# An attention and mixture-of-experts kernel: the experts' rows normalised by GpSimd, turned through memory in 32-column quarters and VectorE's 32x32 transposes, and the first matrices kept on chip

## The reference

```python
x = x + attn(layernorm(x))          # 16 heads, squared scores, causal in chunks of 64, a running state
x = x + ffn(layernorm(x))

# ffn: 8 experts, the best two of the softmax are weighed, but the higher-numbered of them wins
scores = softmax(x @ gate_w + gate_b)
wf = the two largest scores of a token, at their experts, else 0
for i in range(8):
    h = relu(xf * wf[:, i:i+1] @ w1[i] + b1[i])       # w1[i]: 128 x 512
    y = h @ w2[i] + b2[i]                             # w2[i]: 512 x 128
    out = where(wf[:, i:i+1] > 0, y, out)
```

## Time and profile before

| | us |
|---|---|
| median of three runs | 279.69 |
| the profiled run | 279.19 |
| span of its profile | 277.1 |
| PE busy in the span | 256.0 |
| DVE busy | 180.3 |
| ACT busy | 170.3 |
| POOL busy | 165.4 |
| first product of the experts starts | 192.24 |
| granted clock of TensorE, mean | 1.0 of full |

### The profile page before, as it was taken

One profiled execution on the slowest core, in us unless ns is written; L12 is line 12 of the kernel. 1 busy time (PEld: TensorE's weight loads), 2 busy tenths in 40 slices (PEclk: granted clock), 3 DMA queues, 4 the chain that ended last, 5 costly groups with the idle time before them and its releaser, 6 DMA issues.

```text
span 277.1 us, 9167 instructions
## 1 busy us (share of the span) xinstructions
PE 256.0 (92%) x3141; PEld 205.8 (74%) x3141; DVE 180.3 (65%) x726; ACT 170.3 (61%) x297; POOL 165.4 (60%) x190
## 2 busy tenths in 40 slices
PE   0969999999999999999999999788999999999993
PEld 0757677677767777777777777555899899999993
DVE  5472453794776498399299479768878855555552
ACT  2366676767666767676767676564565565656550
POOL 6074444563668596686674775782287775545454
PEclk9999999999999999999999999999999999999999
DMA  5789999999600000000000000065676479877400
GB/s 149 217 297 311 358 361 358 356 332 359 229 21 12 12 22 4 19 22 2 22 13 11 22 7 15 22 190 147 155 225 178 120 187 263 251 214 191 147 31 8
DMA packets 31580, 40.58 MB, mean 146 GB/s; under 512 B 3330, under 2 KB 24356, under 8 KB 31536
## 3 DMA queue, kind: packets, MB, share of 16 engines
q1 hardware_dynamic: 29264, 35.76, 42.7%
q0 software_dynamic: 2272, 4.25, 4.4%
HBM read 17.98 MB, written 22.48 MB: 146 GB/s over the span
## 4 chain that ended last, share of the span: by engine, by line
PE 60%; SPq 22%; DMA 5%; ACT 4%; DVE 3%; issue 3%; POOL 2%; ACTq 0%; DVEq 0%; POOLq 0%
PE sc L1015 24%; PE av L1015 17%; SPq L336 15%; PE p L1015 15%; DMA expert_rows<-pad_rows 5%; ACT scores L402 4%; PE p L1018 4%; SPq L314 3%; SPq L330 2%; POOL expert_rows L553 1%; POOL out L566 1%; POOL scores L528 0%; DVE logit L721 0%; DVE stats L697 0%; SPq L328 0%
## 5 line engine op out<-in xcount | busy, mean ns | idle before, releaser
L402 ACT ACTIVATE scores<-sc 128x1536 f32<-128x1536 f32 x64 | 92.9, 1451 | 48.4 <-PE sc L1015 48.4
L528 POOL TENSOR_SCALAR_AFFINE_SELECT scores<-scores 128x1024 f32<-128x1024 f32 x64 | 70.7, 1107 | 46.3 <-ACT scores L402 46.0
L1015 PE MATMUL sc<-q_sb,k_sb 32*128 32x256 f32 (+1 forms) x1024 | 59.8, 347 | 6.8 <-ACT scores L402 5.6
L1015 PEld LDWEIGHTS sc<-q_sb,k_sb 32*128 32x128 f32 x1024 | 46.3, 184 | 22.1 <-ACT scores L402 15.4
L566 POOL DMA_INDIRECT out<-y_sb,xr x39 | 38.7, 993 | 26.7 <-DVE y_sb L956 20.1
L1015 PE MATMUL av<-scores,v_ext 128*32 128x256 f32 (+1 forms) x1024 | 48.9, 329 | 1.0 <-POOL scores L528 0.8
L475 ACT ACTIVATE hT<-sc,b_sb 128x128 f32<-128x128 f32 x78 | 24.5, 364 | 32.8 <-PE sc L1015 32.7
L553 POOL DMA_INDIRECT expert_rows<-rows,slot_i x32 | 32.2, 1008 | 19.8 <-DVE slot_i L805 9.5
L660 DVE TENSOR_SCALAR k_sb<-p,parity 128x512 f32<-128x512 f32 x32 | 22.5, 744 | 32.4 <-PE p L1015 32.4
L1015 PE MATMUL sc<-xwT,w_t 128*128 128x128 f32 x312 | 41.4, 276 | 0.0
L1015 PEld LDWEIGHTS av<-scores,v_ext 128*32 128x32 f32 x1024 | 28.5, 109 | 16.7 <-POOL scores L528 1.6
(11 more groups left out here) (136 smaller groups left out, 330.3 us busy)
## 6 DMA issues: line engine op xcount, KB each, us to landing
expert_rows<-pad_rows SPq DMA_DIRECT2D x11, 1572.0 KB, 17.8
w_t<-in_L_ffn_w SPq DMA_DIRECT2D x39, 256.0 KB, 3.5
xr<-expert_rows SPq DMA_DIRECT2D x39, 65.5 KB, 3.1
rows<-in_L_attn_hidden_states SPq DMA_DIRECT2D x16, 128.0 KB, 2.7
out<-y_sb,xr POOLq DMA_INDIRECT x39, 3.4
b_sb<-in_L_ffn_b SPq DMA_DIRECT2D x1, 512.0 KB, 5.1
expert_rows<-rows,slot_i POOLq DMA_INDIRECT x32, 2.4
wk_sb<-in_L_attn_Wk SPq DMA_DIRECT2D x1, 128.0 KB, 2.8
```

What stands on the lines that cost most here:

```text
L402: nc.scalar.activation(scores[g][:, :, :, :].rearrange("p c a t -> p c (a t)"), sc[:, :, 0:SW], ACT.Square, scale=Q_SCALE).then_inc(square ...
L528: nc.gpsimd.affine_select(out=scores[g][:, :, 0:2, :], in_=scores[g][:, :, 0:2, :], compare_op=ALU.is_ge, fill=0.0, base=0, pattern=[[0, G ...
L1015: return nc.tensor.matmul(o, lhsT=l, rhs=r, start=start, stop=stop)
```

## The change

- The rows are normalised by POOL (`normalise`, now `tensor_scalar`, with 7 buffers `xw`). POOL does tiles 0 to 5 ahead of its late scatters, and then tile t + 6 after the result of tile t.
- SP stores each normalised tile to a new table `turned` in external memory, as four quarters of 32 features (`store_rows`: 128 x 4 pieces of 128 bytes). Once that has landed, SP loads it back with 32 rows by 4 blocks on each partition (`load_blocks`: 128 pieces of 512 bytes). The load of tile t stands behind the store of tile t + 1.
- DVE turns the tile with one transpose of 32x32 blocks (`turn`), two tiles ahead, between `begin_y` and `late_piece`.
- PE's transposes of the rows and ACT's normalising and copying of them are gone.
- One DMA of 2 MB loads all first matrices (`w1_sb`), ahead of the pads. ACT copies the expert's matrix into one of three buffers `w1_t` (`copy_w1`), two tiles ahead.
- `LEAD`, the number of row loads ahead in the second wave, goes from 4 to 6.

```diff
-    XR, W1, Y, XWT = 20, 6, 10, 4
+    XR, W1, Y, XWT, XW, XB = 20, 3, 10, 4, 7, 6
+    turned = nc.dram_tensor("turned_rows", (TILES, D // STRIP, P, STRIP), fp32, kind="Internal").ap()
...
+            sp.dma_start(w1_sb[:, :].rearrange("p (e n) -> p e n", e=E), w1.rearrange("e d n -> d e n")).then_inc(moe_w, 16)
             sp.dma_start(b1_rows[:, :], b1.rearrange("e (c f) -> (e c) f", f=P)).then_inc(moe_w, 16)
...
-            def load_w1(t, e):
-                after(sp, up_done, t - W1 + 1)
-                sp.dma_start(w1_t[t % W1][:, :], w1[bass.ds(e, 1)].rearrange("e d n -> d (e n)")
-                             ).then_inc(w1_in[t % W1], 16)
...
+            def store_rows(t):
+                sp.wait_ge(xw_ready, t + 1)
+                sp.dma_start(turned[t].rearrange("a q j -> q a j"),
+                             xw[t % XW][:, :].rearrange("q (a j) -> q a j", j=STRIP)).then_inc(xw_out[t % XW], 16)
+            def load_blocks(t):
+                sp.wait_ge(xw_out[t % XW], 16 * (t // XW + 1))
+                after(sp, xwT_ready, t - XB + 1)
+                sp.dma_start(xb[t % XB][:, :],
+                             turned[t].rearrange("a (i b) j -> (a i) (b j)", i=STRIP)).then_inc(xb_in[t % XB], 16)
...
             for t in range(WAVE):
                 load_rows(t, row[t])
-                if t in (3, 5):
-                    load_w1((t + 5) // 2, e[(t + 5) // 2])
-            for t in range(W1, WAVE):
-                load_w1(t, e[t])
+            for t in range(WAVE):
+                store_rows(t)
+                if t:
+                    load_blocks(t - 1)
+            load_blocks(WAVE - 1)
...
                     load_rows(n, row[n])
-                    if n == WAVE:
-                        load_w1(t, e[t])
+                store_rows(t)
                 if t > WAVE:
-                    load_w1(t, e[t])
+                    load_blocks(t - 1)
+            load_blocks(TILES - 1)
...
+            def copy_w1(t, e):
+                after(act, up_done, t - W1 + 1)
+                nc.scalar.copy(w1_t[t % W1][:, :], w1_sb[:, bass.ds(e * FF, FF)]).then_inc(w1_ready, 1)
...
             for t in range(TILES):
                 relu_low(t, e[t])
-                if t + 2 < TILES:
-                    copy_xwT(t + 2)
-                if t + 3 < TILES:
-                    normalise(t + 3)
...
+                if t + 2 < TILES:
+                    copy_w1(t + 2, e[t + 2])
...
+            def normalise(t):
+                pool.wait_ge(xr_in[t % XR], 16 * (t // XR + 1))
+                if t >= XW:
+                    pool.wait_ge(xw_out[t % XW], 16 * (t // XW))
+                nc.gpsimd.tensor_scalar(xw[t % XW][:, :], xr[t % XR][:, 0:D], xr[t % XR][:, FACTOR:FACTOR + 1],
+                                        xr[t % XR][:, MEAN:MEAN + 1], ALU.mult, ALU.add).then_inc(xw_ready, 1)
...
+            for t in range(AHEAD):
+                normalise(t)
             scatter(NB - 4)
             norm2_root(NP - 1)
             scatter(NB - 3)
@@
                     scatter(NB - 2)
                     scatter(NB - 1)
                 send_result(t)
+                if t + AHEAD < TILES:
+                    normalise(t + AHEAD)
...
+            def turn(t):
+                dve.wait_ge(xb_in[t % XB], 16 * (t // XB + 1))
+                after(dve, up_done, t - XWT + 1)
+                nc.vector.transpose(xwT[t % XWT][:, :].rearrange("p (i b) -> p b i", i=STRIP),
+                                    xb[t % XB][:, :].rearrange("p (b j) -> p b j", j=STRIP)).then_inc(xwT_ready, 1)
...
+            turn(0)
+            turn(1)
             for t in range(TILES):
                 relu_high(t, e[t])
                 if t:
                     end_y(t - 1)
                 begin_y(t, e[t])
+                if t + 2 < TILES:
+                    turn(t + 2)
                 late_piece(t)
...
-                pe.wait_ge(w1_in[t % W1], 16 * (t // W1 + 1))
+                pe.wait_ge(w1_ready, t + 1)
...
-            transpose_xw(0)
-            transpose_xw(1)
...
-                if t + 2 < TILES:
-                    transpose_xw(t + 2)
```

More of the change, by code:

```diff
@@ L90, in attention_moe_kernel @@
         gb_sb = sb("gb_sb", [P, E])
+        w1_sb = sb("w1_sb", [P, E * FF])
         w1_t = [sb(f"w1_t{i}", [P, FF]) for i in range(W1)]
@@ L177, in attention_moe_kernel @@
         xr = [sb(f"xr{i}", [P, ROWW]) for i in range(XR)]
-        xw = [sb(f"xw{i}", [P, D]) for i in range(2)]
+        xw = [sb(f"xw{i}", [P, D]) for i in range(XW)]
+        xb = [sb(f"xb{i}", [P, P]) for i in range(XB)]
         xwT = [sb(f"xwT{i}", [P, P]) for i in range(XWT)]
@@ L250, in attention_moe_kernel @@
         xw_ready = sem("xw_ready")
-        xwt_done = sem("xwt_done")
+        xw_out = [sem(f"xw_out{i}") for i in range(XW)]
+        xb_in = [sem(f"xb_in{i}") for i in range(XB)]
         xwT_ready = sem("xwT_ready")
@@ L255, in attention_moe_kernel @@
         hT_high = sem("hT_high")
-        w1_in = [sem(f"w1_in{i}") for i in range(W1)]
+        w1_ready = sem("w1_ready")
         b1_done = sem("b1_done")
@@ L264, in attention_moe_kernel @@
         ATTN_WEIGHTS = 3 * 16
-        MOE_WEIGHTS = 3 * 16
+        MOE_WEIGHTS = 4 * 16
         PADS = (REGION // (PADDED * P) + 1) * 16
@@ L349, in load_rows @@
                 sp.dma_start(xr[t % XR][:, :], region[bass.ds(row, P), :]).then_inc(xr_in[t % XR], 16)
-            e = experts(sp, 0)
+            def store_rows(t):
[7 more added lines that the diff above has]
+                             turned[t].rearrange("a (i b) j -> (a i) (b j)", i=STRIP)).then_inc(xb_in[t % XB], 16)
+            sp.wait_ge(table_ready[0], 1)
             row = loaded(sp, row_i[0][0:1, 0:WAVE], E * REGION)
-            for t in range(4):
-                load_w1(t, e[t])
             sp.wait_ge(rows_out[0], 16 * EARLY * PT)
@@ L358, in _ @@
                 load_rows(t, row[t])
-                if t in (3, 5):
-                    load_w1((t + 5) // 2, e[(t + 5) // 2])
-            for t in range(W1, WAVE):
-                load_w1(t, e[t])
-            e = e + experts(sp, 1)
-            LEAD, SOME = 4, 4
+            for t in range(WAVE):
[3 more added lines that the diff above has]
+            load_blocks(WAVE - 1)
+            LEAD, SOME = 6, 4
             def places(t):
@@ L369, in places @@
                 return loaded(sp, row_i[1][0:1, t:min(t + SOME, TILES - WAVE)], E * REGION)
+            sp.wait_ge(table_ready[1], 1)
             row = row + places(WAVE)
@@ L458, in _ @@
                     copy_oT(late)
-            def copy_xwT(t):
-                act.wait_ge(xwt_done, t + 1)
-                after(act, up_done, t - XWT + 1)
-                nc.scalar.copy(xwT[t % XWT][:, :], xw_bank[:, 0:P]).then_inc(xwT_ready, 1)
-            def normalise(t):
-                act.wait_ge(xr_in[t % XR], 16 * (t // XR + 1))
-                after(act, xwt_done, t - 1)
-                nc.scalar.activation(xw[t % 2][:, :], xr[t % XR][:, 0:D], ACT.Identity, bias=xr[t % XR][:, MEAN:MEAN + 1],
-                                     scale=xr[t % XR][:, FACTOR:FACTOR + 1]).then_inc(xw_ready, 1)
+            def copy_w1(t, e):
+                after(act, up_done, t - W1 + 1)
+                nc.scalar.copy(w1_t[t % W1][:, :], w1_sb[:, bass.ds(e * FF, FF)]).then_inc(w1_ready, 1)
             def relu_low(t, e):
@@ L481, in _ @@
             e = experts(act, 0)
-            normalise(0)
-            normalise(1)
-            copy_xwT(0)
-            copy_xwT(1)
+            copy_w1(0, e[0])
             copy_u(NB - 1)
-            normalise(2)
+            copy_w1(1, e[1])
             act.wait_ge(b1_ready, 1)
@@ L563, in _ @@
                 norm1_root(b + 1, slice(b, b + 1))
+            AHEAD = 6
+            def normalise(t):
[4 more added lines that the diff above has]
+                                        xr[t % XR][:, MEAN:MEAN + 1], ALU.mult, ALU.add).then_inc(xw_ready, 1)
             def send_result(t):
@@ L1170, in _ @@
                     transpose_o(late)
-            def transpose_xw(t):
-                pe.wait_ge(xw_ready, t + 1)
-                after(pe, xwT_ready, t)
-                transpose(xw_bank[:, 0:P], xw[t % 2][:, :]).then_inc(xwt_done, 1)
             def go_up(t):
-                pe.wait_ge(w1_in[t % W1], 16 * (t // W1 + 1))
+                pe.wait_ge(w1_ready, t + 1)
                 pe.wait_ge(xwT_ready, t + 1)
```

1 line of the change is left out of this document (removed).

## The result

The changed kernel takes 316.6 us (median of four runs, 313.5 to 317.8) against 280.0 for the kernel before beside it (278.9 to 280.3): 1.130 times as long, with a 95% interval of 1.120 to 1.139. The profiled run took 317.75 us, its span is 316.0.

What follows compares the result with a forecast made beforehand. The prediction took PE, busy 256.0 of 277.1 us, as the bound before, and PE waiting for rows after the change. Its terms summed to 41.8 us; 277.1 + 41.8 + 2.1 gave 321.0 us, range 302 to 342.

Steps and rivals of the forecast that it cites:

- Part 1: Ahead of the pads: the 2.10 MB load of all first matrices delays pads, scatter, mask and PE by 5.9 us.
- Part 2: First expert tile: SP issues 17 row loads before the first store, then store, load and transpose; 9.2 us later.
- Part 3: Tile 5: its load queues behind tile 6's store, which POOL normalises only after scatters and a send; 7.2 us more.
- Part 4: Tiles 5 to 12: DVE with its transpose and gaps needs 2.4 us a tile; 2.7 us more.
- Part 5: Tile 13: its load waits behind tile 14's store, normalised after four more scatters and a send; 5.2 us more.
- Part 6: Tile 17: SP asks for second-wave rows only after issuing tile 16's load, which waits for a store; 6.7 us more.
- Part 7: Tiles 17 to 38: SP's queue of row load, store and load sets 2.2 us a tile; 4.9 us more.
- behind tile 38: End of the kernel: 0.4 us less is left after the last tile, since POOL no longer trails.
- PE's transposes earn nothing: Expert stage: the 5.6 us of transposes that PE loses bring no gain, since PE now waits.
- The quick one: Rival, 17%: stores land in 2.4 us, loads in 1.7, and the matrices' load hides; 304 us.
- The slow store: Rival, 20%: the store's small pieces cost twice as much, 4.4 us a store; 340 us.
- The other side: Rival, 3%: the path through memory stays ahead of PE, so only its lost transposes count; 273.6 us, faster.

Runs made afterwards that it cites:

- e1: Changed kernel with the 2 MB load of first matrices behind the pads in SP's queue, not ahead: 318.9 us, 1.055 times the kernel before.
- e2: Kernel before plus only the 2 MB load of first matrices, which nobody reads, ahead of the pads: 306.0 us against 301.95, ratio 1.015.
- e12: Kernel before with only the rows' path through memory, first matrices still loaded tile by tile: 323.0 us against 279.3, ratio 1.153.
- e11: Kernel before with only the one load of first matrices and ScalarE's copies, rows on their old path: 283.3 us against 279.3, ratio 1.013.
- e7: Changed kernel with all 17 first-wave tiles normalised ahead of the late scatters, eight ahead from then on: 310.4 us, 1.029 times the kernel before.
- e3: Changed kernel with GpSimd normalising eight tiles ahead instead of six, nine buffers xw: 308.3 us, 1.023 times the kernel before.
- e5: Changed kernel with matmuls whose results nobody reads ahead of tiles 0, 5 and 13 on TensorE: 321.1 us against the changed kernel's 323.05.

## Why the prediction came out, term by term

| place | predicted | measured |
|---|---|---|
| Part 1, to the experts' start | 5.9 | 7.8 |
| Part 2, tile 0 | 9.2 | 6.4 |
| Part 3, tile 5 | 7.2 | 7.4 |
| Part 4, tiles 5 to 12 | 2.7 | 4.4 |
| Part 5, tile 13 | 5.2 | 4.6 |
| to tile 17 (0.4 and Part 6) | 7.1 | 3.6 |
| Part 7, tiles 17 to 38 | 4.9 | 4.7 |
| behind tile 38 | -0.4 | 0.0 |
| sum | 41.8 | 38.9 |

The measured column is the difference of the chain rows above from the earlier trace rows, each less what had been lost ahead of it (tile 5: 225.26 - 203.57 - 14.26 = 7.4). The time, 316.6, is 4.4 below the 321, and inside the range.

- **Part 1.** The pads are 5.3 late (5.9 said); e1 and e2 show the cause, and both came out below the 7.8 of the table. The other 2.5 us are PE's clock: it had waited 5.7 us for the mask, and 16 weighing matmuls then take 1.51 us, where 32 take 1.44 later in the chain. From their start to PE's second group of scores it takes 6.7 us (87.52 to 94.23), where the same work took 4.2 before (82.21 to 86.39), and PE waits for nothing in between. No term of mine had this.
- **Part 2.** Right in its order (17 issues, then a store), wrong in two terms. One is the store's price: it lands after 1.84 and not 3.2 us. I took 3.2 from a slope over transfers that ran beside others. With the matrices' loads beside it a store does take 2.7 (e12). I let the emptier queue shorten the load back (2.2 for 3.1) and not the store: that is the error. The other term I had at nothing: the first row load starts 4.31 us after the last early scatter before (186.79 and 182.48), and 2.46 now (192.75 and 190.29), so 1.9 us come back. The four loads of first matrices that stood between them are gone; e11, without them, has 2.51, and e12, with them, 3.94. Against this the 17 issues took 9.3 us and not 8.8.
- **Parts 3 and 5.** Right in mechanism and size. GpSimd normalises tile 6 at 221.32 behind scatters and a send, 216.8 + 5.9 in my count; e7 takes that order away and the stall ahead of tile 5 goes.
- **Part 4.** 1.7 short: the first two groups of matmuls from tile 5 on run at half clock (2.04 and 1.91 us), and tile 9 waits for a load back that takes 3.54 us (issued at 232.13), where I had 2.2.
- **Part 6.** 3.5 us too dear. With Part 1's 5.9 I had the first store of the second wave at 260.0 and the load back behind its landing at 263.2; the store went at 258.13 and the load at 260.20. So the queue was less far behind than I had it, and the store was cheaper.
- **Part 7.** The size is right by luck, the mechanism is wrong. I let the load back wait for its store and made that the period. It waits 1.7 us in all from 262 to 309 us; what binds is the loop over three tiles. I expected PE to wait at every second tile; the chain has it waiting at tiles 20, 23, 26, 28, 31, 34 and 37, nearly every third. I had worked out a loop through GpSimd, as 9.6 us over five tiles, and called it hidden. It counts three, since the load of a tile is issued behind the store of the next, and since VectorE's turn stands ahead of the older tile's relu and result. Two tiles more of lead (e3) bring the pace from 2.2 to 1.9, and e7's to 1.82.
- **PE's transposes earn nothing.** True while PE waits; e7 shows them earned as soon as it does not.
- **The rivals.** The quick one had the right store (1.9, said 2.4) but also an early experts' start and PE-bound tiles, and both were missing. The slow store falls with the 1.9 us of the changed kernel's own store. GpSimd's normalise takes 0.46, nearer to 0.3 than to 1.06. The other side needed stores more than four tiles ahead of PE. e7 has them behind tile 17, where PE does set the pace, but not ahead of it.

The errors nearly cancel, and that is luck. Parts 2 and 6 were 6.3 us too dear. The slow clock, at four places, was left out altogether: 2.5 us behind the pads, and by e5's profiled run about 4.3 from tile 0 on.

## What to carry to other kernels

A stage that goes through memory costs little by its transfers (1.9 and 2.2 us here) and much by the order in which in-order engines reach it: write down the loop from a result's send back to the same engine's next turn, with the number of tiles that it really spans, before calling it hidden. Give such a path its lead first: two tiles more gave back 14 us, a store in four times fewer pieces nothing that could be told. And where a change makes PE wait for some us at a time, add what PE's lower clock costs behind each wait.

## What the runs showed of the hardware

- TensorE's granted clock fell to half behind idle stretches of 7.4, 7.0 and 4.0 us (eight matmuls in 2.05 us, not 0.9 to 1.1). With useless matmuls in those stretches (e5) it stayed at full. Behind shorter ones it went both ways: it stayed at full behind 2.32 us in the changed kernel (1.00 from 262 to 265 us) and fell, a little later, behind 2.28 in e5 (0.57 from 267 to 270) and 2.84 in e1 (0.57 from 86 to 90).
- A store of 64 KB in 512 pieces of 128 bytes landed after 1.9 us, in 128 pieces of 512 bytes after 1.7, on another chip; beside loads of 256 KB in the same queue the first took 2.7 (e12).
- VectorE turns 128x128 float32 in 32x32 blocks in 0.405 us; GpSimd multiplies and adds over 128x128 in 0.44.
- The same VectorE instruction took 1.03 us while GpSimd's masks ran (201.37 to 205.65) and 0.19 later. VectorE's timeline in e7:

```profile
202.55 1.03 DVE L737 TENSOR_TENSOR logit<-scaled,gb_sb 128x32 f32<-128x32 f32 x1
...
226.09 0.19 DVE L737 TENSOR_TENSOR logit<-scaled,gb_sb 128x32 f32<-128x32 f32 x1
```
